# Moving the router's counts, the expert list and the expert tiles to other slots of a hand-ordered decoder layer

## What is computed

```python
x = layernorm(x + sparse_attention(x))       # 8 heads, 96 keys of at most 256 for each query, picked by an index score
x = layernorm(x + retention(x, ctx, ctx))    # 16 heads of 8, decay masks
x = layernorm(x + moe(x))                    # router: softmax over 8 experts, the best 2
# moe: relu(x @ w1[e] + b1[e]) @ w2[e] + b2[e], weighted by the two router probabilities
```

## Time and profile before

| what | us |
|---|---|
| median of three timed runs | 766.42 |
| the three runs | 762.03, 766.42, 773.82 |
| the profiled execution, its own time | 757.35 |
| span of its instructions | 755.5 |

### The profile page before, as it was taken

The page is one execution under the profiler, slowest core; times in us unless marked ns, Lnnn a source line. Parts: engine busy times, 40 slices in busy tenths (PEclk is TensorE's granted clock), DMA queues, the critical chain, the costliest instruction groups (busy, mean ns, idle before and its releaser), DMA issues.

```text
span 755.5 us, 18822 instructions
## 1 busy us (share of the span) xinstructions
PE 644.0 (85%) x6549; PEld 495.8 (66%) x6549; DVE 473.1 (63%) x1733; ACT 369.5 (49%) x1271; POOL 274.7 (36%) x451
## 2 busy tenths in 40 slices
PE   5469988997999899988998999889977997567794
PEld 4245664675577677755686777757766776457794
DVE  1618647876985797578766975687744674314334
ACT  4335445453565476544554766355533643234352
POOL 0345602911840163139701540179622001342053
PEclk9857598897799999965899999968986998669998
DMA  4080030020306330303044416040523222248760
GB/s 150 1 299 2 2 106 1 2 107 1 124 3 204 108 97 19 111 16 129 9 170 127 116 41 195 23 144 17 172 86 101 87 82 64 87 138 267 227 214 26
DMA packets 43413, 73.23 MB, mean 97 GB/s; under 512 B 7664, under 2 KB 31544, under 8 KB 42168
## 3 DMA queue, kind: packets, MB, share of 16 engines
q1 hardware_dynamic: 41528, 68.36, 28.7%
q0 software_dynamic: 1792, 3.67, 1.5%
HBM read 61.69 MB, written 10.32 MB: 95 GB/s over the span
## 4 chain that ended last, share of the span: by engine, by line
PE 44%; issue 10%; POOL 9%; DVE 8%; ACT 3%; DMA 1%; POOLq 0%; DVEq 0%
PE bM L830 6%; PE bG L975 5%; PE bH L1185 5%; PE bR L1202 4%; PE bM L1018 3%; PE bS L994 3%; PE bM L1023 2%; POOL sorted_tokens L780 2%; PE bR L1107 2%; PE bW L1247 2%; PE bS L991 2%; PE bC L830 2%; PE bC L1124 2%; PE bW L1202 1%; PE bC L1075 1%
## 5 line engine op out<-in xcount | busy, mean ns | idle before, releaser
L1385 ACT ACTIVATE pp<-pp,nmx 128x224 f32<-128x224 f32 x96 | 46.4, 483 | 79.5 <-DVE nmx L1662 78.1
L1668 DVE TENSOR_TENSOR gs<-bG,rank_t 96x512 f32<-96x512 f32 x96 | 65.5, 682 | 18.5 <-PE bG L975 18.5
L1467 ACT ACTIVATE ht<-bH,wt 128x128 f32<-128x128 f32 x192 | 54.7, 369 | 39.1 <-PE bH L1185 39.1
L1397 ACT COPY pts<-bM 128x256 f32<-128x256 f32 x96 | 35.4, 369 | 63.0 <-PE bM L830 62.7
L1731 DVE TENSOR_TENSOR sm<-bC,cst 128x512 f32<-128x512 f32 x64 | 43.6, 681 | 34.0 <-PE bC L1124 33.6
L1202 PE MATMUL bR<-wt,ht 128*128 128x128 f32 x328 | 51.1, 305 | 15.8 <-DVE taken L1808 13.3
L726 POOL TENSOR_TENSOR r<-x,cst 128x256 f32<-128x256 f32 x8 | 5.8, 724 | 153.7 <-DVE x L1695 153.7
L975 PE MATMUL bG<-oh,kspl 128*96 128x512 f32 x160 | 61.3, 467 | 0.0
L1202 PEld LDWEIGHTS bR<-wt,ht 128*128 128x128 f32 x328 | 46.9, 215 | 21.2 <-issue 15.1
L1185 PE MATMUL bH<-xt,wt 128*128 128x128 f32 x384 | 56.6, 295 | 4.1 <-DVE xt L1855 2.0
L1650 DVE TENSOR_SCALAR ppn<-pp,rls 128x224 f32<-128x224 f32 (+1 forms) x128 | 49.8, 389 | 14.1 <-DVE rls L1647 0.5
(11 more groups left out here) (288 smaller groups left out, 1595.9 us busy)
## 6 DMA issues: line engine op xcount, KB each, us to landing
wt<-in_experts SPq DMA_DIRECT2D x64, 578.0 KB, 4.1
sidx<-far_slots SPq DMA_DIRECT2D x8, 1536.0 KB, 7.0
xs<-sorted_tokens SPq DMA_DIRECT2D x56, 64.0 KB, 3.7
expert_rows<-ot SPq DMA_DIRECT2D x56, 64.0 KB, 3.5
sorted_tokens<-acc SPq DMA_DIRECT2D x11, 256.0 KB, 7.8
cst<-shape_constants SPq DMA_DIRECT2D x1, 1603.5 KB, 6.3
xn<-in_x SPq DMA_DIRECT2D x8, 128.0 KB, 4.9
xr<-in_x SPq DMA_DIRECT2D x8, 128.0 KB, 3.2
```

The lines of the kernel that those rows point to most:

```text
L1385: AC(pp[:, s % 2, 0:w], bS[:, 0:w] if s < T0 else pp[:, s % 2, :], ACT.Exp, scale=1.0 if s < T0 else -1.0, bias=nmx[:, s % 2:s % 2 + 1], a ...
L1467: last = AC(ht[:, t % 2, f, :], w[:, 128 * f:128 * f + 128], ACT.Relu, bias=wt[:, t % NW, FF + f:FF + f + 1])
L1668: TT(gs[:, g % 2, :].rearrange("p (t j) -> p t j", j=FAR), bG[0:96, :].rearrange("p (t j) -> p t j", j=FAR), rank_t[:, :].rearrange("p (o ...
```

## The change

- The counts go from slot 18 to 17.5 on PE, and `place` and `taken` on DVE from slot 19 to 17.5, right behind the router.
- The expert list goes from slot 2 to slot 0. POOL's rotation of `rqn` goes from slot 1 to slot 0, ahead of the list's scatters.
- Expert tiles start in slot 4 instead of 8 of their step, and the slot 17 of `TILE_SLOTS` becomes 11. A group is thus done two tile slots earlier; step 8 holds entries 14 and 15 of group (3, 4) instead of 12 to 15.
- Near tile 1 of the attention has its scores in bank `bG`, which the gathers use only from slot 3 on. So scores of tile 1 wait for no exponential, and those of tile 2 only for tile 0's. The first gather waits for tile 1's exponential.
- The final moments (`means`) come 5 slots after the gather's point, or 13 where that would be a slot below 4 or above 15. By `plan` they move for batch 0 from (step 4, slot 7) to (4, 6), batch 1 from (6, 15) to (6, 9), batch 2 from (6, 19) to (6, 13), batch 3 from (8, 13) to (8, 8), batch 4 from (8, 17) to (8, 12), each normalisation one slot later. Gathers: batch 0 (3, 19) to (3, 13), 1 (6, 7) to (6, 4), 2 (6, 11) to (6, 8), 3 (8, 5) to (8, 3), 4 (8, 9) to (8, 7).

```diff
-TILE_SLOTS = (0, 2, 4, 5, 8, 10, 13, 15, 17)
-LIST_SLOT, FIRST_SLOT = 2, 6
-MEAN_LATE = 8
+TILE_SLOTS = (0, 2, 4, 5, 8, 10, 11, 13, 15)
+LIST_SLOT, FIRST_SLOT = 0, 4
...
-            for table, late in ((gather, 0), (first, 3), (second, MEAN_LATE), (third, MEAN_LATE + 1)):
-                table[step + (s + late) // NS, (s + late) % NS] = n
+            mean = NS * step + s + 5
+            if mean % NS > 15 or mean % NS < 4:
+                mean += 8
+            for table, here in ((gather, NS * step + s), (first, NS * step + s + 3), (second, mean), (third, mean + 1)):
+                table[here // NS, here % NS] = n
...
+        def near_bank(tile):
+            return bG if tile == 1 else bS
...
-                if s == 3:
+                if s == 2:
                     pool.wait_ge(c_x1.sem, c_x1.at(i.n, 1))
                     pool.wait_ge(r_k.sem, r_k.at(i.n, 1))
                     rotate(rqn[:, :, :], x1[:, :, :], "cos_q", "sin_q", r1, r2, r_q)
...
                 pe.wait_ge(g_out.sem, g_out.at(i.n, g))
+                if g == 0:
+                    pe.wait_ge(s_exp.sem, s_exp.at(i.n, 2))
...
+                elif tile == 1:
+                    pe.wait_ge(g_out.sem, g_out.at(i.n - 1, 12))
                 else:
-                    pe.wait_ge(s_exp.sem, s_exp.at(i.n, tile))
+                    pe.wait_ge(s_exp.sem, s_exp.at(i.n, tile if tile > 2 else 1))
...
-                if s == 2 and i.n != DENSE:
+                if s == 1.5 and i.n != DENSE:
 
                     pe.wait_ge(r_m.sem, r_m.at(i.n, 1))
...
-                if s == 3 and i.n != DENSE:
+                if s == 1.5 and i.n != DENSE:
 
                     dve.wait_ge(r_full.sem, r_full.at(i.n, 2))
```

6 lines of the change are left out of this document (3 added, 3 removed).

## The result

| | before | changed |
|---|---|---|
| median, us | 762.03 (5 runs, 761.32 to 773.82) | 784.52 (5 runs, 780.63 to 791.07) |
| ratio, 95% interval | | 1.0278 (1.0224 to 1.0331): slower |
| profiled run, us (span) | 757.35 (755.5) | 780.63 (778.8) |

The forecast was 765.5, from 750 to 780. The time lies above the range. The first view is the page of the changed kernel: busy time by engine, the clock in forty slices and the core's line.

What follows compares the result with a forecast made beforehand. PE was taken as the bound, but from T to the first far tile DVE and GpSimd. Terms 6 + 15 - 15 + 1 - 6 = +1 us; 764.2 plus 1.3 gave 765.5, range 750 to 780.

Steps and rivals of the forecast that it cites:

- Step 1: S to T, seven step ends: PE stands 1.85 us for `hot` at 17.5, T at S + 5.25; +6 us.
- the part on the clock: Whole span: the change makes as many gaps as it closes, so zero in the sum, 10 us either way in the range.
- Step 2: Slots 8 to 15: 8.5 expert tiles move in at 1.8 us each; +15 us, from 13 to 20.
- Step 3: T to the first far tile: near bank, ready `taken`, moved moments and early list shorten it; -15 us, 7.5 in step 7.
- rival B: Slower by the clock: a 4.2 us PE gap in list steps, plus 1.85 at 17.5, loses full clock; 780 us, chance 0.2.
- without a gap: Step 3 of the kernel before: DVE works unbroken from 255.99 to 266.12, up to the first masked retention product.
- Step 4: Batch 1's final moments in slot 9 of step 6: DVE may stand 0 to 6 us, one slot of slack; +1 us.
- Step 5: Tail: first row flip at T + 20.7, 10.3 us earlier, against 4.3 us PE cost from batch 3's moments; -6 us.
- Rival A: Faster: gaps between T and slot 4 close in full if DVE has slack there; 745.5 us, half gives 755; chance 0.25.

Runs made afterwards that it cites:

- o: Kernel before with near tile 1's scores in the gathers' bank and VectorE's counts in slot 18 instead of 19, TensorE's unchanged: 746.31 us, 0.989 of before.

## Why the prediction failed, by its own steps

**Step 1, counts at 17.5: wrong by 12 us, the term that failed most.** The wait was seen rightly: `hot` at S + 2.6, PE standing 2.0 (forecast 1.85). T was to be at S + 5.25 and is at S + 6.6 to 7.5. With the gap filled, T is at S + 4.9 to 5.5 in six of seven ends and the sum is +7.1 us over before, against the forecast of +6. What the step left out is the speed of what follows: the output matmuls at 2.0 us, from the earlier trace rows at full clock, took 3.2 to 3.8 behind the gap. That price stood among the unknowns of the part on the clock, at zero and "10 either way", though the step itself had made seven gaps. (Two small slips do not matter: T was at S + 3.65 at the end of step 3 before, so 1.6 and not 1.8 was to be added there, and the sum of +1 went into the forecast as 1.3.)

**Step 2, the tiles' slots: the sum met by luck.** +15 forecast, and +1 for the moments of part 4; +16.1 measured. A tile in slot 11 costs 2.0 us, 1.8 was forecast. But the steps under this sum are not as forecast:

| first far tile to S, step | 2 | 3 | 4 | 5 | 6 | 7 |
|---|---|---|---|---|---|---|
| forecast (moments in 6) | +5.4 | -3.6 | +5.4 | +1.8 | +5.3 | +1.8 |
| measured | +2.6 | +4.0 | -1.4 | +1.9 | +6.6 | +1.9 |
| length times clock | +6.0 | -1.4 | +8.1 | +1.9 | +11.2 | +1.9 |

Before, step 4 had a mean clock of 0.80, step 6 of 0.85 and step 3 of 1.00; in the changed kernel they have 0.97, 0.94 and 0.90. So at one and the same clock the signs are those of the forecast and the sum is 27.6 and not 16: 9.3 us of new standing, which the forecast had at 1, and some 18 us of work for 15. A term that the forecast had put at zero, the clock, took 12 of it back.

In step 3 there is a wait beside the clock. GpSimd's gather waits 18.44 us for the store of the first group's last tile, and the rotation and split of the keys behind it reach PE late:

```profile
317.25 1.02 POOL L773 DMA_INDIRECT gb<-expert_rows,slot  x1 [18.44 <-DMA expert_rows<-ot]
...
327.49 1.09 PE L835 MATMUL bC<-cst,rks 128*128 128x128 f32 x4 [3.16 <-DVE rks L1577]
```

That wait is 15.49 us before, 23.43 in the run of slot 11 alone, whose step 3 lost but 1.6 us. So it is a cause that was read from one trace, not one that was shown.

**Step 3, T to the first far tile: right in direction, -8.9 instead of -15.** Step 7 gave 8.5 (7.5 forecast), for the reason given. The list steps 2, 4 and 6 were to give 5.3 and gave 0.7. PE has the gap that rival B had drawn (4.2 us), 3.0, 4.0 and 4.4 us long, and the stretch begins at the low clock: `xT,iwq` 1.65 us for 0.90. How much of the miss is clock is open: of the 60.2 us of these three stretches 36.9 are at the low level, and of before's 60.9 it was 28.5. Steps 1, 3 and 5 lost 1.8 us and were to win 1.7. The 1.5 us won from the start to step 0's first far tile are within its spread (61.6 to 65.5 us between the profiles). And "without a gap" was not quite so: in the same stretch of step 3 DVE had stood 0.50 us for `pp` at 261.03, and was busy for 9.56 of 10.81 us.

**Step 4, moments of batch 1: mis-sized.** +1 forecast; 3.8 to 6.3 us measured against the run with the moments back, 1 to 2 of them by length times clock. (They stand five slots behind the gather's, not three, as the forecast had it.) DVE's stand of 2.62 us was inside "0 to 6 us", but the slack of one slot did not hold it. The run with the moments back is 15 us faster than the changed kernel, the run of the moments alone 0.997 of before. They cost only beside the other parts, and by more than their own wait: what lies between is clock.

**Step 5, the tail: -2.1 instead of -6.** The first row flip came at T + 22.3 (20.7 forecast), 8.8 us earlier than before; 6.7 of it went again until the end. With 122.2 and 117.2 us in the two later profiles, whether the tail won anything is open. DVE stood 1.0 us for the sum, not 5; instead the weight load goes out late, and PE stands 2.75 us. The timeline of SP's queue shows what is ahead of it, the store of batch 3's final rows, five slots earlier than before (that it is the cause is read from this order, not tried); in the next fence PE's row:

```profile
697.37 0.44 SPq L600 DMA_DIRECT2D expert_rows<-ot  x1
701.29 0.39 SPq L633 DMA_DIRECT2D out<-acc  x1
701.87 0.34 SPq L586 DMA_DIRECT2D wt<-in_experts  x1
```

```profile
705.99 1.13 PE L1194 MATMUL bH<-xt,wt 128*128 128x128 f32 x8 [2.75 <-issue]
```

**The clock and rival B.** Of rival B (0.2, 780) the time came near and the mechanism happened, in another place than it named: not at the 4.2 us gap of the list steps but at 17.5, seven times, which it called an addition. But B took the low clock as a loss in sum, and in sum it hardly grew; that its 780 is near 784.5 is in part luck. The rule quoted from the Trainium skill (TensorE: Matmul & The Clock Gate, HAM oscillation), that idle gaps put the clock down and the work behind runs slowly, agrees with the filled and the unfilled kernel, 2.05 against 3.78 us. The argument against it failed. It was that slots 4 to 6 of step 5 ran at full clock although PE had stood for `taken` shortly before. That observation was true, and it was one of five. It also lies 14 us behind that wait. And in step 6, the stretch set against it, the level had risen to 2.4 GHz again behind the wait for `taken`, and fell anew where PE stood 1.98 us for `sm`. The five waits for `taken` in before, with what stands right behind each:

```profile
253.83 1.13 PE L1202 MATMUL bR<-wt,ht 128*128 128x128 f32 x8 [2.21 <-DVE taken L1808]
...
406.95 1.13 PE L1202 MATMUL bR<-wt,ht 128*128 128x128 f32 x8 [2.22 <-DVE taken L1808]
...
560.92 2.04 PE L1202 MATMUL bR<-wt,ht 128*128 128x128 f32 x8 [3.19 <-DVE taken L1808]
...
639.54 2.04 PE L1202 MATMUL bR<-wt,ht 128*128 128x128 f32 x8 [3.49 <-DVE taken L1808]
```

Behind two of them PE stayed at full clock (1.13 us), behind the other two shown and that at 481.56 it did not (2.04). A list of all five would have spoken for a price and not against one. In the changed kernel it was every gap for `hot`, save that in step 3 the level was low already; why there always and here three times of five, no run settles. The mean clock could not show the loss: 0.868 before, 0.869 after, since the time at the low level (twice the span times what the mean lacks of 1) only went from 199 to 204 us. It changed its place: from S to T it is 37.1 us for 1.5, from far tile to S 44.8 for 75.8. So about what the boundary lost by the clock, the full part of the steps got back, and the sum of the loss is standing:

| PE stands, us | before | changed | moved |
|---|---|---|---|
| S to T, seven ends | 0.1 | 14.3 | +14.2 |
| T to the first far tile | 63.0 | 56.7 | -6.3 |
| first far tile to S | 12.3 | 23.6 | +11.3 |
| last T to the end | 36.2 | 38.3 | +2.1 |

The first line is the wait that step 1 had foreseen (13 us). The others were to be -15, +1 and -6. So beside the speed behind the gap, these three are what the forecast had wrong, and the experiments do not take them apart any further.

**Rival A** (faster) asked whether DVE has slack at the boundary. The near bank alone, 1.001, says it returns nothing of the 11.9 us. The early list alone, 0.977, says that a gain of the size of A's was there to be had, though not by A's reason: 9.6 us of it are a higher clock from far tile to S. The forecast priced the parts as a sum, and no part at more than its own length. What fell out of that is the cover: step 1 noted the 2.4 us of tile that had covered the router, as a saving of matmul time at the boundary, not as what kept PE running.

## What to carry to other kernels

When an edit takes work out of a place and another puts a wait into it, price the pair: slot and counts made no gap, or two, alone, and seven together. Beside the length of a part, read its mean clock: length times clock nearly added over the parts here (11 and 15 us, 28 to 31 together), and the lengths themselves did not. Give every new gap on TensorE a range from its length alone to its length and the work right behind it at the slow level's duration, and look at the instruction directly behind all gaps that the trace has, not behind one. Where counts or another small product come late, move the consumer's half earlier (here one slot of VectorE, 0.989), and keep the waiting matmul behind the work that sets the path.

## What the runs showed of the hardware beyond the forecast

- Waits of 1.8 to 2.4 us on TensorE were followed by the 1.2 GHz level in all 21 cases of three profiles of the changed kernel: the output matmuls in 3.2 to 3.8 us for 2.02 to 2.05. In 18 the level fell during the wait or within 0.9 us of its end, in three it had been low before. Independent matmuls of equal length in the wait's place kept the level at 2.4 GHz where it was there already; where it was not (step 3), they ran in 3.78 us and the work behind them in 2.05.
- Waits of 0.3 to 0.4 us for `ot` in the same place (counts alone, tile back in slot 17) had no such effect: 2.05 us behind each. There an expert tile stood just ahead. With slot 17 empty, 0.4 us for `ots` was followed by 3.25, 2.74 and 2.53 us and once by 2.02 (slot 11 alone, counts back), and with no wait right before them the output matmuls took 2.67 to 2.82 once in each of five profiles (step 3 of before, near bank, moments and o, step 4 of slot 11). Of before's five waits of 2.2 to 3.5 us for `taken`, two of 2.2 had none either.
- One kernel's profiles differ by up to 4.5 us in one step (53.9, 54.2 and 58.4 us in step 4) with the same waits at its ends, and before's medians by 15 us between stretches of runs. A comparison of two single traces carries that with it.
